# A prologue in another order, and embedding rows fetched by GpSimd one round ahead

## The reference

```python
emb = where(tokens < 64, concat(color_W[t // 16], shape_W[t % 16 // 4], quantity_W[t % 4]),
            special_W[clip(tokens - 64, 0, 5)])            # t = min(tokens, 63)
h0  = emb * sqrt(192) + positional_encoding                # (2, 2048, 192)
h   = h0 + mixer(norm(h0))          # in_proj, causal conv of 4 taps, silu, a state-space scan
                                    # over 24 heads of 16 with state 64, gate silu(z), out_proj
h1  = h + (silu(v @ w_gate) * (v @ w_up)) @ w_down         # v = rmsnorm(h), inner width 768
out = h1 + shared expert + 2 of 8 routed experts of layernorm(h1)   # inner width 128
```

## Time and profile before

| | |
|---|---|
| median of 3 runs | 807.42 us (805.93 to 807.51) |
| the profiled execution, its own time | 805.65 us |
| its span in the trace | 803.5 us |
| busy, share of the span: PE / DVE / ACT / POOL | 95% / 80% / 68% / 35% |
| mean granted TensorE clock | 0.992 of full speed |
| DMA | 16.77 MB, all issued by SyncE |

### The profile page before, as it was taken

The page is one execution under the profiler, slowest core; times in us unless marked ns, Lnnn a source line. Parts: engine busy times, 40 slices in busy tenths (PEclk is TensorE's granted clock), DMA queues, the critical chain, the costliest instruction groups (busy, mean ns, idle before and its releaser), DMA issues.

```text
span 803.5 us, 23139 instructions
## 1 busy us (share of the span) xinstructions
PE 767.3 (95%) x7374; PEld 655.2 (82%) x7374; DVE 643.7 (80%) x1712; ACT 549.0 (68%) x1228; POOL 284.5 (35%) x427
## 2 busy tenths in 40 slices
PE   3679999999999999999999999999999999999897
PEld 2447888888888888888888888888888888888786
DVE  5699987879788787978878797887889788786745
ACT  4975776767677676767767676776767777676533
POOL 2254342423434242343324234332423433242122
PEclk9899999999999999999999999999999999999999
DMA  7410010000000000000000000000000000000000
GB/s 244 164 66 2 1 26 2 7 19 6 18 0 24 0 6 18 6 18 0 24 0 6 18 3 21 0 21 3 6 18 3 21 0 17 7 6 11 3 1 20
DMA packets 13475, 16.77 MB, mean 21 GB/s; under 512 B 1986, under 2 KB 12104, under 8 KB 13000
## 3 DMA queue, kind: packets, MB, share of 16 engines
q1 hardware_dynamic: 13448, 16.43, 6.4%
HBM read 12.23 MB, written 4.19 MB: 20 GB/s over the span
## 4 chain that ended last, share of the span: by engine, by line
PE 86%; DVE 3%; issue 1%; ACT 1%; POOL 0%; POOLq 0%; DVEq 0%; ACTq 0%
PE bank L1540 39%; PE bank L1932 11%; PE bank L1859 8%; PE bank L1715 5%; PE bank L1704 5%; PE bank L1828 4%; PE bank L1815 3%; PE bank L1806 2%; PE bank L1792 2%; PE bank L1644 1%; DVE mr L1176 1%; PE bank L1568 1%; PE bank L1649 1%; PE bank L1688 1%; PE bank L1899 1%
## 5 line engine op out<-in xcount | busy, mean ns | idle before, releaser
L1176 DVE SCALAR_TENSOR_TENSOR mr<-er,gm 128x512 f32<-128x512 f32 x192 | 126.0, 692 | 5.2 <-ACT er L753 3.5
L753 ACT ACTIVATE er<-bank 128x512 f32<-128x512 f32 x192 | 106.0, 596 | 18.3 <-PE bank L1704 17.7
L1932 PE MATMUL bank<-w2t,w_raw 128*128 128x192 f32 x576 | 112.6, 327 | 0.4 <-DVE w_raw L1345 0.4
L843 ACT ACTIVATE sg<-bank 128x256 f32<-128x256 f32 x144 | 55.1, 383 | 62.3 <-PE bank L1540 51.4
L1115 DVE SCALAR_TENSOR_TENSOR xa<-xr,cw_,xa 128x256 f32<-128x256 f32 x192 | 92.4, 488 | 6.1 <-ACT xa L661 4.5
L1932 PEld LDWEIGHTS bank<-w2t,w_raw 128*128 128x128 f32 x576 | 91.0, 190 | 1.8 <-DVE w_raw L1438 0.7
L792 ACT ACTIVATE sg<-bank 128x256 f32<-128x256 f32 x90 | 34.3, 381 | 65.5 <-PE bank L1540 46.4
L1540 PE MATMUL bank<-x_h,w_hi 128*128 128x256 f16 x288 | 78.6, 273 | 0.0
L1540 PE MATMUL bank<-x_h,wt_lo 128*128 128x256 f16 x288 | 78.7, 273 | 0.0
L1540 PE MATMUL bank<-x_h,w_lo 128*128 128x256 f16 x288 | 78.6, 273 | 0.0
L1540 PE MATMUL bank<-x_l,w_hi 128*128 128x256 f16 x288 | 78.6, 273 | 0.0
(11 more groups left out here) (244 smaller groups left out, 2162.1 us busy)
## 6 DMA issues: line engine op xcount, KB each, us to landing
out<-w_raw SPq DMA_DIRECT2D x16, 192.0 KB, 2.0
pos<-position SPq DMA_DIRECT2D x16, 96.0 KB, 2.9
ri<-exponent_rows SPq DMA_DIRECT2D x1, 1536.0 KB, 6.4
w_raw<-weights SPq DMA_DIRECT2D x1, 1156.0 KB, 5.5
wt_raw<-weights SPq DMA_DIRECT2D x1, 1156.0 KB, 8.8
tok<-tokens SPq DMA_DIRECT2D x16, 70.0 KB
sums<-lj SPq DMA_DIRECT2D x16, 64.0 KB, 1.9
w2t<-w SPq DMA_DIRECT2D x1, 864.0 KB, 11.3
```

Source lines behind the costliest of these rows:

```text
L753: act.activation(er[:, r % NER], p_d[r % 2][:].rearrange("p (h i) -> p h i", h=HG), ACT.Exp)\
L843: act.activation(sg[:, e % 4, :], src[e][:, 0:NB * Q], ACT.Silu).then_inc(sx_ready, 1)
L1176: ve.scalar_tensor_tensor(mr[:, r % NMR], er[:, r % NER], 1.0, gm[:, r // NQ, :].unsqueeze(1).to_broadcast([128, HG, Q]), ALU.min, ALU.mult)\
L1932: ins = pe.matmul(p_ex[e][:, b * D:(b + 1) * D], hh[:, e % NHH, b * Q:(b + 1) * Q], w2t[:, e, :], start=True, stop=True)
```

## The change

1. The embedding is a gather. The host stores the tokens as (2048 + 128) x 2, the last 128 rows zero. SyncE loads 128 x 2 tokens, one position per partition; GpSimd clips them to row numbers and issues two indirect DMAs, one per batch row, that fetch 128 table rows of 768 bytes each into `emb`; VectorE makes h0_next = emb * sqrt(192) + position in one operation that reads SBUF. `tab3`, `onehot`, `pre_embed` and the preparation of the table are gone. In a round of the loop GpSimd issues `embed(p + 1)`, between `pre(p)` and `norm2(b)`, so the rows are fetched one round before they are read; SyncE loads the tokens of block p + 1. The last fetch, of block 16, reads the zero rows and is not used.
2. The ramp has another order on every engine, and TensorE first runs 50 matmuls of 128 x 128 on the identity, whose result nobody reads.
3. `convolved_first` and `convolved_rest` wait for the last skip matmul (`xs_skipped`) in place of the last masked one, and `second_scan`, which only the ramp calls, has its three skip matmuls together.

```diff
 # SyncE
-            def load(c):
-                if later(c):
-                    sp.wait_ge(onehot_ready, c)
+            def load_tokens(c):
+                if later(c):
+                    sp.wait_ge(row_ready, c)
                 settle(sp)
-                sp.dma_start(tok[:], tokens[:, bass.ds(c * Q, Q)].partition_broadcast(V)).then_inc(tokens_in, 16)
+                sp.dma_start(tok[:], tokens[bass.ds(c * Q, Q), :]).then_inc(tokens_in, 16)
+            def load_position(c):
                 if later(c):
                     sp.wait_ge(h0_ready, c)
...
             def body(p, f, b):
                 if p is not None:
-                    load(p)
+                    load_tokens(p + 1)
+                    load_position(p)
                     sums_in_rows(p)
...
             def ramp():
-                load(1)
+                load_tokens(1)
+                load_position(1)
                 load_rows()
                 load_columns(slice(COL_G, COL_E), in_mid)
+                load_tokens(2)
                 sums_in_rows(0)
...
-            sp.dma_start(ids[:], vocab_ids).then_inc(in_first, 16)
-            sp.dma_start(tab[:], table).then_inc(in_first, 16)
-            load(0)
+            load_tokens(0)
+            load_position(0)
 # GpSimd
+            def embed(c):
+                pool.wait_ge(tokens_in, c * 16 + 16)
+                if later(c):
+                    pool.wait_ge(emb_in, c * 32)
+                settle(pool)
+                pool.tensor_scalar(row[:], tok[:], float(V - 1), 0.0, ALU.min, ALU.max).then_inc(row_ready, 1)
+                pool.wait_ge(row_ready, c + 1)
+                if later(c):
+                    pool.wait_ge(h0_ready, c)
+                settle(pool)
+                for b in range(NB):
+                    pool.indirect_dma_start(emb[:, b, :], None, table, bass.IndirectOffsetOnAxis(row[:, b:b + 1], 0))\
+                        .then_inc(emb_in, 16)
...
             def ramp():
+                embed(0)
+                pool.memset(state[:], 0.0).then_inc(setup_p, 1)
...
                 keep(0)
                 pre(0)
+                embed(1)
                 pre(1)
+                embed(2)
                 steps_decay(0)
...
                 if p is not None:
                     pre(p)
+                    embed(p + 1)
                 norm2(b)
 # ScalarE
-                    act.wait_ge(yq_done, c * NR)
+                    act.wait_ge(xs_skipped, c)
...
                 gates(0, 1)
+                operands(0, p_pair[1])
                 gates(0, 0)
-                operands(0, p_pair[1])
...
                 on_channels(0)
-                middle_weights(0)
                 exponentials(0, range(4))
                 convolved_in(1, 1, p_out)
                 first_tap(1, 1)
+                middle_weights(0)
                 exponentials(0, (4, 5))
 # VectorE
-                ve.wait_ge(in_first, 48)
-                ve.tensor_scalar(tab_rest[:, 0, :], tab[:], EMB_SCALE, None, ALU.mult).then_inc(setup_v, 1)
...
-            def pre_add(c, src=p_misc):
-                ve.wait_ge(emb_done, c + 1)
+            def pre_add(c):
+                ve.wait_ge(emb_in, c * 32 + 32)
...
-                ve.tensor_tensor(h0_next[:], src[:, 0:NB * D].rearrange("p (b d) -> p b d", b=NB),
-                                 pos[:].unsqueeze(1).to_broadcast([128, NB, D]), ALU.add).then_inc(h0_ready, 1)
+                ve.scalar_tensor_tensor(h0_next[:], emb[:], EMB_SCALE, pos[:].unsqueeze(1).to_broadcast([128, NB, D]),
+                                        ALU.mult, ALU.add).then_inc(h0_ready, 1)
...
                 pre_split(1, p_pair[0][:, NB * Q:2 * NB * Q])
+                operands(0, p_pair[1])
                 taps(0, 3)
-                operands(0, p_pair[1])
...
                 masked_g(0)
+                taps(1, 0)
                 masks(0, range(4))
                 from_state(0, 0)
-                taps(1, 0)
+                taps(1, 1)
                 masks(0, (4, 5))
-                taps(1, 1)
                 new_state(0, 0)
                 scanned(0, 0)
+                taps(1, 2)
                 masks(0, (6, 7))
-                taps(1, 2)
+                taps(1, 3)
                 masks(0, (8, 9))
...
                 scanned(0, 1)
-                taps(1, 3)
                 new_state(0, 1)
...
-                if p is not None:
-                    pre_onehot(p)
                 swiglu(b, p, f)
 # TensorE
+            def warm_up(n):
+                pe.wait_ge(setup_a, 1)
+                for _ in range(n):
+                    pe.matmul(p_y[:, 0:128], id16[:], id16[:], start=True, stop=True)
...
                 pe.wait_ge(y_sum[0], c + 1)
-                skipped_x(1, 0)
+                for k in range(KT):
+                    skipped_x(1, k)
...
                     mlp_gate_up(c, f, p_pair[f % 2])
-                    if f == 1 and p is not None:
-                        pre_embed(p)
...
             def ramp():
-                pe.wait_ge(in_first, 48)
-                pre_embed(0)
+                pe.wait_ge(in_first, 16)
+                warm_up(50)
                 pre_turn(0, p_misc, p_pair[1][:, 0:NB * Q])
-                pre_embed(1, p_out[0])
```

More of the change, by code:

```diff
@@ L28 @@
 I32 = mybir.dt.int32
+U32 = mybir.dt.uint32
 NB = 2
@@ L99, in reached, with program @@
         return c * self.per + self.n
-def program(nc, tokens, position, vocab_ids, table, weights, norms, conv_w, conv_b, shared_rows, d_skip, w_out, w_down,
+def program(nc, tokens, position, table, weights, norms, conv_w, conv_b, shared_rows, d_skip, w_out, w_down,
             w2, identity, lower_ones, triangle_rows, exponent_rows, pair_rows, spread_rows, out):
@@ L145, in program @@
         mhalf = sb("mhalf", [128, 2])
-        tok = sb("tok", [V, NB, Q], I32)
+        tok = sb("tok", [128, NB], I32)
+        row = sb("row", [128, NB], U32)
+        emb = sb("emb", [128, NB, D])
         pos = sb("pos", [128, D])
-        onehot = sb("onehot", [V, NB, Q], BF16)
         h0_next = sb("h0_next", [128, NB, D])
@@ L261, in program @@
         tokens_in, position_in = sem("tokens_in"), sem("position_in")
-        onehot_ready, emb_done, h0_ready, stat_ready, r0_ready = (sem(n) for n in (
-            "onehot_ready", "emb_done", "h0_ready", "stat_ready", "r0_ready"))
+        row_ready, emb_in, h0_ready, stat_ready, r0_ready = (sem(n) for n in (
+            "row_ready", "emb_in", "h0_ready", "stat_ready", "r0_ready"))
         uc_ready, uh_ready, ul_ready, uh_turned, ul_turned, u_hi_ready, u_lo_ready = (sem(n) for n in (
@@ L614, in _ @@
             run(pool, ramp, body, finale)
+            pool.wait_ge(emb_in, 32 * (NC + 1))
         @block.scalar
         def _(act):
-            act.wait_ge(in_first, 48)
+            act.wait_ge(in_first, 16)
             act.copy(id16[:], idf[:]).then_inc(setup_a, 1)
@@ L1461, in ramp @@
                 pre_split(0, p_pair[1][:, 0:NB * Q])
-                pre_add(1, p_out[0])
+                pre_add(1)
                 pre_stats(1)
@@ L1556, in turn @@
                 ins.then_inc(low_turned, 1)
-            def pre_embed(c, dst=p_misc):
-                if not later(c):
-                    pe.wait_ge(setup_v, SETUP_V)
-                pe.wait_ge(onehot_ready, c + 1)
-                if later(c) and dst is p_misc:
-                    pe.wait_ge(s_ready[0], c)
-                settle(pe)
-                for b in range(NB):
-                    for k in range(3):
-                        ins = pe.matmul(dst[:, b * D:(b + 1) * D], onehot[:, b, :], tab3[:, k, :],
-                                        start=(k == 0), stop=(k == 2))
-                ins.then_inc(emb_done, 1)
+            def warm_up(n):
+                pe.wait_ge(setup_a, 1)
+                for _ in range(n):
+                    pe.matmul(p_y[:, 0:128], id16[:], id16[:], start=True, stop=True)
             def pre_turn(c, dst=p_misc, low=p_out[1][:, NB * Q:2 * NB * Q]):
@@ L1574, in pre_turn @@
                     pe.wait_ge(setup_a, 1)
+                    pe.wait_ge(setup_v, SETUP_V)
+                elif dst is p_misc:
+                    pe.wait_ge(s_ready[0], c)
                 turn(c, dst, low, u_t, uh_ready, ul_ready, uh_turned, ul_turned)
@@ L1752, in second_scan @@
                     sums()
-                skipped_x(1, 1)
                 masked(c, (8, 9))
@@ L1791, in skipped_x @@
             def skipped_x(b, k):
-                pe.matmul(p_y[:, k * Q:(k + 1) * Q], skip[:, k], xs[:, k, b, :], start=(k == 0), stop=False,
-                          skip_group_check=True)
+                ins = pe.matmul(p_y[:, k * Q:(k + 1) * Q], skip[:, k], xs[:, k, b, :], start=(k == 0), stop=False,
+                                skip_group_check=True)
+                if b == NB - 1 and k == KT - 1:
+                    ins.then_inc(xs_skipped, 1)
             def state_read(c, b, p):
@@ L2123 @@
 N_ROWS = 2
-SETUP_V = 9
+SETUP_V = 4
 SETUP_P = 7
@@ L2173 @@
     arrays = {
```

(2 more changed lines are left out.)

38 lines of the change are left out of this document (8 added, 30 removed).

## The result

The changed kernel takes 810.58 us (median of 5 runs, 810.08 to 811.18); the kernel before, beside it on the same chip, 807.26 (805.93 to 807.51). The ratio is 1.0052, 95% interval 1.0041 to 1.0063: slower, and outside the range of the prediction. The profiled executions stand further apart (span 808.8 against 803.5): the one of the kernel before took 805.65, less than any of those five runs. Its median beside the later experiments was 805.7 to 805.9, so the time of the profiled execution is a usual one.

A forecast was written before the change was run, and what follows sets the result against it. TensorE looks busy, but the loop is bound by ScalarE's Silu and VectorE's gt, the embedding filling a hole. Loop 0.1, start -0.4, tail 0.95, first round 0.4: 807.42 - 1.05 = 806.4 us, range 803.0 to 809.2.

The forecast's parts named there:

- The loop: Loop rounds: removing 7.4 us of embedding from TensorE wins only 0.1, since the third feed-forward tile waits for gt.
- Rival A: TensorE is the bound, so all 7.4 us of the loop are won: 799.1 us; chance 0.07.
- Part (c): Start, GpSimd: embed(2), waiting for the third tokens, delays steps_decay(0) to 22.2, 0.9 later than before.
- rival C: Slower: a gather holds GpSimd about 2 us, delaying steps_decay(0) and the second block: 809.6 us; chance 0.16.
- Part (a): Start: table preparation and one-hot leave VectorE, second gather issued near 5, so block 0's h0_next comes at 7.9, 1.1 earlier.
- Part (b): Start: fifty matmuls raise TensorE's clock, half counted; with the earlier h0_next, the first projection ends some 1.5 us earlier.
- Gather price: GpSimd: each gather takes 1.1 us (bounds 0.54 and 2.12), so embed takes 2.4 (1.3 to 4.5).
- the sentence beside rival C: Skill rule: VectorE's two-port modes lock ports GpSimd needs for DMA descriptors, so a gather beside them would come later.
- Part (d): Start, new order: GpSimd's end to first exponential takes 9.1 instead of 9.56; exponentials at 34.9, 0.4 lost.
- The tail: Ramp's end: second block's transposes 1.45 earlier and 0.5 shorter, 1.0 lost through rm; gives 0.95 (0 to 2).
- rival D: The order does nothing; GpSimd's casts and rm take the whole tail: 807.4 us; chance 0.12.
- Rival B: Gathers cost 0.54 each and tokens land at 18.5; start gives about 1.9, tail 2.0: 803.5 us; chance 0.20.

The follow-up runs named there:

- a1_filler: Changed kernel with six idle matmuls of 192 columns put back where the embedding stood in TensorE's loop stream; 810.91 us, ratio 1.0063.
- a5_ramp: Changed kernel; in the ramp third tokens load first, the 3 MB bulk only after block 1's gathers landed, embed(2) behind steps_decay(0); 804.96 us, ratio 0.9994.
- a4_embed2: Changed kernel with one edit: on GpSimd embed(2) stands behind steps_decay(0); 809.19 us, ratio 1.0044.
- d2_cold: d1_both without the fifty warm-up matmuls on TensorE; 799.56 us, ratio 0.9920.
- d1_both: a5_ramp plus, in the loop, ScalarE's exponential er6 of the other block moved ahead of the cast v_h; 799.20 us, ratio 0.9918.
- d3_two: d1_both with block 1's tokens, row numbers and rows in own buffers, gathers right behind block 0's, memsets on VectorE; 798.80 us, ratio 0.9909.
- b2_order: Kernel before with only the new ramp order on ScalarE, VectorE and TensorE, without gather or fifty matmuls; 805.89 us, ratio 1.0000.
- c1_before_er6: Kernel before with ScalarE's seventh exponential of a block moved ahead of the cast v_h; 804.79 us, ratio 0.999.
- b1_skip: Kernel before with the second batch row's three skip matmuls moved from behind the state read to right behind the embedding; 813.73 us, ratio 1.0097.
- a3_bulk: Changed kernel with SyncE issuing the 3 MB of exponent rows and middle weights only after blocks 0 and 1's gathers landed; 815.65 us, ratio 1.0123.

## Why the prediction was wrong

**The loop: right.** The embedding was filler. The forecast booked 0.1 of 7.4 us; the period stayed, the wait for gt took its place (forecast 0.5, bracket 0.36; from the last matmul ahead of it, at 269.21, it is 0.63 to the tile's start, 0.52 more than the usual 0.11), and a1_filler shows it from the other side. Rival A falls. Norm2 was not held up: `embed` ends 3.80 us before GpSimd's next work in a loop round, and 0.96 before it in the first.

**Part (c), "what decides is GpSimd": this step failed.** It let `embed(2)` and the third tokens set steps_decay(0), at 22.2, and gave rival C "0.5 to 1" for block 1. Its mistake was the landing of block 1's rows, which stands in its sum at nothing. It followed the third tokens behind the bulk, with the 9.2 us of the earlier trace rows, but not block 1's gathers, which shared the DMA engines with the same 3 MB. The rows took 5.1 to land, and with them `dx`, which stands behind the sum on VectorE, came 4.8 late; steps_decay(0) started at 27.17 in place of 22.2. a5_ramp and a4_embed2 price the two parts: 3.9 to 4.2 for the bulk in the way, 1.4 to 1.7 for `embed(2)`. The third tokens were later than forecast (21.4 against 19.5 to 20, since the bulk left at the same time as before and not 1.5 earlier), but nobody waited for them: GpSimd came to them at 23.69, right behind `pre(1)`, and `pre(1)` itself waited for VectorE.

**Part (a): wrong by its whole gain.** The tokens came earlier than assumed (2.83 against 3.6), but between the row numbers and the first gather lie 0.97 us, the first gather takes 1.21 and 0.30 pass behind it, so the second starts at 5.50 and not near 5. From there to the sum at 9.04 it is 3.54 us in place of 2.9, with the DMA engines 86% busy from 4 to 9 us by the first weights. So block 0's sum is where it was.

**Part (b): wrong.** Half of the clock's gain was booked; d2_cold shows none at the projections. The forecast took the idle time between the fifty and the first work for 2 us; it is 3.4. The granted clock fell to 0.50 of full speed near 12.9, just ahead of the first work at 13.04; in d1_both it fell near 13.5, behind the first transposes. The Trainium skill says that activity releases the clock (TensorE: Matmul & The Clock Gate, Part 1); the same section lists idleness as what brings the lower rate back, and the forecast's sentence on it used only the first half. The rows of d1_both agree with both: the first transposes, 3.25 us behind the fifty, took 0.27 where d2_cold took 0.37, and the projections from 15.72 on took 0.42 as in d2_cold.

**Gather price: right where it counted.** 1.1 us each was assumed; 0.95 to 1.21 measured in the ramp and in the loop, but `embed` took 3.5 to 3.8 in all against 2.4, as the gaps of 0.85 and 0.30 had not been thought of. In the first round, `body(2, 1, 0)`, the two gathers took 2.94 and 1.81:

```profile
85.89 2.94 POOL L458 DMA_INDIRECT emb<-table,row  x1 [0.86 <-POOL row L452]
...
86.50 1.35 DVE L1049 TENSOR_TENSOR wt_lo<-wt_raw,wt_hi 128x1156 f16<-128x1156 f32 x1
```

No other gather has VectorE's operations of 128x1156 beside it, and none took over 1.21; a5_ramp, d1_both and d3_two show the same 2.94 and 1.81 there. Whether VectorE held GpSimd up there, as the sentence beside rival C has it for other modes of VectorE, no experiment tried. It cost nothing here, since GpSimd was idle for 0.96 us behind the second one. Rival C named the right side and both true items, but its price per gather (2.12) and its point of decision (1.6) were wrong: the kernel got slower at 1.1. That its 809.6 is near the measured 810.58 is luck: 2.4 for the gathers and 0.5 to 1 for block 1 stand where 1.4 to 1.7 and 3.9 to 4.2 were measured.

**Part (d): too short.** From steps_decay(0)'s start to the first exponential 3.6 + 9.1 = 12.7 us were forecast; it is 13.7 in b2_order and a5_ramp and 14.1 in the changed kernel. The last Silu of the convolution waits for the last taps, as the forecast had said (it starts 1.28 later behind GpSimd's end). But of the 1.98 to be saved behind it only 0.73 came: the gate of 0.4 still stands ahead of that Silu, and ScalarE now waits for TensorE, 0.36 before `bt` and 0.28 before the exponential (a5_ramp), where it had waited 0.16 in all. With all of this the first exponential is 27.17 + 14.09 = 41.26 in place of 34.9.

**The tail: right in number, by luck.** 0.94 us from the first exponential to the first v_h, 0.95 forecast. But 2.90 us were won up to the operation behind the first transposes (VectorE's `xd`, at 57.55 before and at 61.46), not 1.95, and 1.96 were given back behind it, not 1.0, and not through `rm`. ScalarE's v_t did wait for rm, but was done at 73.19, while VectorE, which has no idle time from `xd` on, came to its own v_t only at 73.97. Its operations took 12.51 from `xd` to v_t in place of 10.55. The largest difference is in `wt_lo`, first before, then after, with GpSimd's cast beside it, which took longer than the 2.12 us of the earlier trace rows too:

```profile
62.00 2.05 DVE L1030 SCALAR_TENSOR_TENSOR wt_lo<-wt_raw,nrm,wt_hi 128x1536 f16<-128x1536 f32 x1
```

```profile
64.03 3.64 POOL L583 CAST wt_hi<-wt_raw 128x2312 f16<-128x2312 f32 x1
...
65.95 3.32 DVE L1041 SCALAR_TENSOR_TENSOR wt_lo<-wt_raw,nrm,wt_hi 128x1536 f16<-128x1536 f32 x1
```

GpSimd's xw products were 1.07 shorter in return (3.59 against 4.66), so that from the first cast to rm it was 9.21 in place of 8.76. Nor is the tail a gain of the order: part (d) of the new order is 0.6 us longer, b2_order measures nothing in sum, and against c1_before_er6's 33.42 the new order's tail of 33.92 is a loss. The base was not as firm as the earlier trace rows looked, since the old order makes up 1.3 us of a late start: three profiled executions with its ramp had the first exponential at 34.27 (b1_skip), 34.45 and 35.74 (c1_before_er6). To that extent rival D was right: the order does nothing. Rival B needed gathers of 0.54 and the third tokens at 18.5; neither came.

What stays open: why the second of the two last casts on GpSimd took 3.64 us where it took 2.12 before. It and VectorE's `wt_lo` grew together, in b2_order and a5_ramp too, but which held up which was not tried; nor was the tie of the 1.3 us to TensorE's rate. The last 0.5 us of the table were not looked into.

## What to carry to other kernels

A transfer that was fetched ahead in the loop, where nobody waited for it, was on the critical path in the ramp. List there every small transfer with what is already queued on the DMA engines, and issue bulk loads behind the last small one that an early engine waits for. The work of an engine that looks 100% busy may still be filler; take the work out and shorten the chain that it covered in the same edit. Here the first alone left the period at 47.19, the second alone gave 0.05 us a round, and both gave 0.39, which with the repaired ramp makes 805.75 into 799.20 us. Where a matmul has been taken from a full engine, the first thing to look for is the wait that it had hidden. And where a time is forecast from one execution's row, look at the same row in a second one: the first exponential of the old order came anywhere from 34.27 to 35.74.

## What the runs showed of the hardware

An indirect DMA of 128 rows of 768 bytes held GpSimd for 0.95 to 1.21 us, with 0.30 between two of them and 0.84 to 0.97 between the operation that writes the row numbers and the first one (0.27 for block 1 in d3_two). So two gathers occupied it for 3.5 us, of which 2.1 were the gathers' own. Beside VectorE's operations of 128x1156 two gathers took 2.94 and 1.81 us. They landed 1.6 to 1.8 us after issue with quiet DMA engines (a5_ramp: 15.76 to 17.55, DMA share 0.25), 2.6 beside the first weights (block 0 of the changed kernel: 6.45 to 9.04) and 5.1 behind 3 MB at a DMA share of 0.92; a token load of 1 KB behind the same bulk took 8.8 to 8.9 (a3_bulk: 19.99 to 28.84; the changed kernel: 12.54 to 21.4).

After fifty matmuls in 5.49 us and 3.25 us without work the first transposes ran at full rate (d1_both: 0.27 against 0.37 in d2_cold), the granted clock then fell to 0.50, and the projections from 15.72 on took 0.42. In the two kernels, which differ in the fifty alone, the full rate came at 18.77 without them and after 20.04 with them. Before its first recorded change the column of the granted clock says nothing: in d2_cold it reads 1.00 from 16 to 18 us, while matmuls of 256 columns took 0.42.
